# Identity matmuls into an unused bank while TensorE waits, ahead of the expert slots and in the return from them

## What is computed

```
x = x + tanh(g_xattn[0]) * L0_xattn(layernorm(x), ctx, ctx)    # retention, 2 heads
x = x + tanh(g_ffn[0])   * L0_ffn(layernorm(x))                # 8 experts, the best one of each token
x = x + tanh(g_xattn[1]) * L1_xattn(layernorm(x), ctx, ctx)    # 32 heads in 8 groups, causal softmax
x = x + tanh(g_ffn[1])   * L1_ffn(layernorm(x))                # silu(gate) * up, 2 of 4 kept, down
```

## Time and profile before

| | us |
|---|---|
| median of 3 runs | 377.06 (376.61 to 378.37) |
| profiled execution, own time | 379.09 |
| its span, first to last instruction | 377.3 |
| mean granted clock of TensorE | 0.946 of full |
| TensorE busy | 327.8 (87% of the span) |
| VectorE busy | 241.5 (64%) |
| ScalarE busy | 161.4 (43%) |
| GpSimd busy | 102.3 (27%) |

### The profile page before, as it was taken

How to read it: one execution, slowest core, us unless ns; L and a number is a source line. 1 busy time by engine, 2 the same in 40 slices (tenths; PEclk the granted TensorE clock), 3 DMA queues, 4 the chain that set the end, 5 groups by cost and what they waited for, 6 DMA issues and landing times.

```text
span 377.3 us, 4821 instructions
## 1 busy us (share of the span) xinstructions
PE 327.8 (87%) x1526; PEld 208.4 (55%) x1533; DVE 241.5 (64%) x564; ACT 161.4 (43%) x333; POOL 102.3 (27%) x154
## 2 busy tenths in 40 slices
PE   3999785587999727999899999989899999999997
PEld 1485674476888515555544644643534444445885
DVE  4368876683554467889937984992442459778911
ACT  2534361534233312237867665865863233333000
POOL 7203663540000376301441334333450001000000
PEclk9999998578999955999999999999999999999999
DMA  7997000135111126300000000000000000000011
GB/s 247 373 415 202 0 16 2 51 96 174 43 57 56 58 72 232 143 0 7 2 7 0 3 0 9 0 1 9 0 2 1 0 0 2 0 0 0 30 42 42
DMA packets 14025, 22.56 MB, mean 60 GB/s; under 512 B 2049, under 2 KB 11393, under 8 KB 13186
## 3 DMA queue, kind: packets, MB, share of 16 engines
q1 hardware_dynamic: 13234, 20.16, 15.5%
q0 software_dynamic: 768, 2.10, 1.7%
HBM read 15.96 MB, written 6.03 MB: 58 GB/s over the span
## 4 chain that ended last, share of the span: by engine, by line
PE 62%; DVE 19%; ACT 6%; issue 5%; DMA 3%; POOL 3%; SPq 1%; another core or an unknown queue 0%; DVEq 0%; ACTq 0%; POOLq 0%
PE bank L260 46%; DVE mx L1289 6%; PE bank L475 5%; PE bank L443 4%; ACT region L965 3%; PE bank L446 2%; PE bank L276 2%; DVE stats L1035 2%; PE bank L270 2%; ACT s_high L925 1%; POOL rstd L738 1%; DVE x_sb L1075 1%; PE bank L490 1%; DMA x_sb<-in_x_dram 1%; DVE sact L1255 1%
## 5 line engine op out<-in xcount | busy, mean ns | idle before, releaser
L965 ACT ACTIVATE region<-bank,padcol 128x512 f32<-128x512 f32 x96 | 62.4, 695 | 18.1 <-PE bank L260 17.3
L1289 DVE TENSOR_REDUCE mx<-bank 128x2 f32<-128x512 f32 (+1 forms) x96 | 61.3, 684 | 11.2 <-remote 6.3
L260 PE MATMUL bank<-xT,e_gu 128*128 128x512 f32 x128 | 57.6, 594 | 0.5 <-ACT xT L819 0.5
L802 POOL TENSOR_SCALAR_AFFINE_SELECT region<-region 128x1024 f32<-128x1024 f32 x32 | 35.0, 1095 | 81.5 <-ACT region L965 81.4
L260 PE MATMUL bank<-qst,kblk 128*128 128x512 f32 x96 | 46.0, 489 | 0.7 <-DMA qst<-nmT 0.3
L443 PE MATMUL bank<-kblk,qst 128*128 128x512 f32 x96 | 44.5, 482 | 1.6 <-ACT qst L910 0.8
L260 PEld LDWEIGHTS bank<-xT,e_gu 128*128 128x128 f32 x128 | 23.3, 190 | 25.1 <-issue 24.3
L446 PE MATMUL bank<-causb,identb 128*128 128x256 bf16 (+1 forms) x89 | 28.4, 319 | 0.0
L260 PE MATMUL bank<-e_down,region 128*128 128x256 f32 x128 | 27.8, 379 | 0.0
L1075 DVE SCALAR_TENSOR_TENSOR x_sb<-bank,tg,x_sb 128x256 f32<-128x256 f32 x24 | 11.6, 483 | 25.0 <-PE bank L260 24.9
L734 POOL TENSOR_SCALAR veps<-mv 128x1 f32<-128x1 f32 x40 | 10.8, 271 | 61.4 <-DVE mv L1037 59.3
(11 more groups left out here) (177 smaller groups left out, 630.7 us busy)
## 6 DMA issues: line engine op xcount, KB each, us to landing
e_gu<-in_e_gu_dram SPq DMA_DIRECT2D x2, 1408.0 KB, 12.1
x_sorted<-zero SPq DMA_DIRECT2D x1, 1920.0 KB, 9.2
y_sorted<-region SPq DMA_DIRECT2D x15, 128.0 KB, 1.7
x_sb<-in_x_dram SPq DMA_DIRECT2D x4, 256.0 KB, 4.1
ctxT<-in_ctxT_dram SPq DMA_DIRECT2D x2, 512.0 KB, 6.1
e_down<-in_e_down_dram SPq DMA_DIRECT2D x1, 1024.0 KB, 13.9
region<-x_sorted SPq DMA_DIRECT2D x1, 1024.0 KB, 7.5
e_gu<-in_f_gate_dram SPq DMA_DIRECT2D x1, 1024.0 KB, 4.9
```

The lines of the kernel that those rows point to most:

```text
L260: return pe.matmul(dst, lhsT, rhs, start=first, stop=last)
L802: pool.affine_select(out=block, in_=block, compare_op=ALU.is_ge, fill=0.0, base=0, pattern=[[0, 2], [0, PER_GROUP], [1, P]], channel_multi ...
L965: taken(act.activation(dst, src.rearrange("p (h n) -> p h n", n=SEQ - mt * P), ACT.Exp, bias=padcol[:, key:key + 1], scale=float(HD) ** -0 ...
L1289: taken(dve.reduce_max(mx[:, b % 2, nt, quads, q, hg], src, AX), "sa")
```

## The change

A helper `stay_warm` multiplies the identity by the mask, 512 columns, into a bank that no stage uses at that point, so many times; nothing reads the result. It is called in seven places of TensorE's program, with three waits ahead of it. No other engine's program changes.

```diff
+            def stay_warm(bank, n):
+                for _ in range(n):
+                    pe.matmul(banks[bank][:, :], identb[:, :], causb[:, :, :], start=True, stop=True)
...
             pe.wait_ge(sem("routed"), 4)
+            pe.wait_ge(sem("res0_taken"), TILES)
+            stay_warm(7, 7)
             slot_turn(0)
             slot_turn(1)
             pe.wait_ge(sem("gu_split"), 4)
+            stay_warm(7, 4)
             expert = [slot_gate_up(0)]
...
             keys(1, "main")
-            for n in range(QUERIES_AT, QUERIES_AT + 6, 2):
+            pe.wait_ge(sem("sx_taken"), SLOTS)
+            pe.wait_ge(sem("sa_t_taken"), SLOTS)
+            stay_warm(5, 34)
+            for n, gap in ((QUERIES_AT, 2), (QUERIES_AT + 2, 2), (QUERIES_AT + 4, 5)):
                 queries(0, n)
+                stay_warm(5, gap)
             for piece in range(2):
                 stack_piece(0, piece, "main")
+            stay_warm(5, 3)
             for n in range(24):
                 scores(0, n)
```

## The result

The changed kernel took 375.69 us (median of 14, 374.49 to 376.68). The kernel before, run beside it 14 times, took 379.29 us (376.61 to 380.06). The ratio is 0.992 (0.9898 to 0.9942): 3.0 us gained, 2.2 to 3.9 by the interval. Two of the three runs shown ahead of the prediction (376.61, 377.06, 378.37) were among the shortest of this kernel: in all 101 of its timed executions in this study the median was 379.4, and 8 stayed under 377.1.

A forecast was written before the change was run, and what follows sets the result against it. TensorE, 62% of the chain's span, was taken to bound it, at half clock in two places. Terms 1.3 + 3.05 = 4.35 us took the median 377.06 to 372.7, forecast as 373.0; range 371.5 to 375.8.

The forecast's parts named there:

- rival 2: Return: the clock is down again when the queries come, so term 2 is 0; 375.8 us, chance 0.08.
- the sum: Whole kernel: term 1 plus term 2, 1.3 + 3.05 = 4.35, say 4.4 us gained.
- the allowance: From 372.7 to 373.0: a median execution may pay a little less for the clock than the profiled one.
- term 1: Entry of the slot loop: full clock brings the third slot product 1.3 us earlier; bounds 0 and 1.4.
- term 2: Return from the experts: low parts 1.85 us earlier plus 1.2 at the row maxima, 3.05; bounds 1.85 and 3.3.
- The cover of the 34: Return: the 34 matmuls end at 137.4, 0.3 us before the first normalized tile at 137.70.
- the prediction's own signs: Wrong if the 34 end after the first tile; right if no clock under full from 130 to 155.
- Rival 3: Identity products don't hold the clock; the 34 end 5.3 us behind the first tile; 383.4 us, chance 0.06.
- point of decision: TensorE's order before the return's first transpose: it turns slower from 0.24 us per added matmul.
- The price of a matmul: Each added 512-column matmul: 0.23 us at full clock; bounds 0.21 and 0.46.
- the load of slots 2 to 6: Entry: needed by 88.7, there by 88.0, so nothing to pay; cover only 0.7 us.
- just don't bind: Return: the last gathers have landed by 145.2, and residual 6 would want them at 145.6.

The follow-up runs named there:

- return only: Kernel before plus only the return's added matmuls (34, 2, 2, 5, 3), none at the entry; 376.51 us, ratio 0.993.
- block-only kernel: Changed kernel without the 2, 2, 5 and 3 matmuls between the return's steps; the 34 and the entry stay; 376.19 us, ratio 0.991.
- block of 20: Changed kernel with 20 in place of 34 added matmuls in the return; 376.11 us, ratio 0.9926.
- dense tail: Changed kernel with 6 of the 34 matmuls moved ahead of the next batch's keys; 376.06 us, ratio 0.9917; run again 375.55 us, ratio 0.9912.
- block of 58: Changed kernel with 58 in place of 34 added matmuls in the return; 381.4 us, ratio 1.004.
- warm start, first: Changed kernel plus 16 matmuls of zeros by zeros at the start (8 and 2 of 256 columns, 6 of 128); 375.92 us, ratio 0.9905.
- kernel before, again: The kernel before, unedited, run again for the clock of each execution; 379.57 us, ratio 1.0002.

## Why the prediction was wrong in size

The forecast was 373.0 us; 375.69 was measured. It went the way that was forecast and by the mechanism forecast, but the time is 2.7 us off and outside the 371.8 to 374.0 that was given a chance of 0.70. That it lies in the range is luck: the slow end, 375.8, was put there for rival 2, and rival 2 (the clock down when the queries come) did not happen.

**The step that failed** is the last one: "From the median the sum gives 372.7", and then 0.3 more. The median of the three runs, 377.06, is not where this kernel lies: it was 379.0 to 379.6 in every later set, 379.29 beside the changed kernel. Of the 2.7 us, 2.2 come from this base; the sum was 0.75 too large against the medians, and the allowance took 0.3 of that back. The profiled execution's own 379.09, which the text called 2.0 above the median, was an ordinary one; from it the sum had given 374.7. The spread of the three runs was read as a small allowance, when it said that the median could be off by about as much.

**The sum** itself holds in the profile: term 1, 1.3, measured 1.09; term 2, 3.05, measured 3.16. But term 2 agrees in part by luck: the low parts began 1.48 us earlier after the keys, not 1.85, the first row maximum 1.62 and not 1.9, and from there to the negation 1.54 were gained, not 1.2. On the runs the sum is 3.0 to 3.6 us, not 4.35. Two things that the profiles show can make it smaller. The entry's fall isn't in every execution (return only, 5.58 without its matmuls). And the fall near the block can be longer: 75.35 in place of 73.8 for the block-only kernel, whose program is the changed kernel's up to the end of the block. How often each comes was not counted, so that they account for the difference is not shown.

**The cover of the 34** was wrong, and by two of the prediction's own signs it was wrong here: the clock was under full between 130 and 155, and the 34 ended after the first tile, by 0.95 us. "No row shows the clock falling while TensorE works without a gap" was no protection: the earlier trace rows had a mean of 0.59 in a microsecond in which TensorE was busy throughout, after a gap, and in the return it fell at the loose products ahead of the block. Little of the 0.95 reached the end, since the low parts waited only 0.37 us: VectorE's residuals 2 and 3 were the cover, as in the prediction. Rival 3 had this place and its point of decision; its price needed the clock to stay down, and it came back while the added matmuls ran in each of the six profiles with a fall.

**The price of a matmul** was taken as 0.23. Measured, 28 took 6.22 us, 0.22 each, and 0.43 at half clock (131 to 133). The Trainium skill, page "TensorE: Matmul & The Clock Gate", section "Back-to-back issue gap", gives 216 ns for the isolated matmul and 131 ns in a sustained stream of pairs. The trace agrees with the first and not with the second, in a stream of just such pairs.

**The loose products.** The same page, section "A second HAM failure mode: psum-queue depth-cycling", says that short idles between groups of matmuls can bring the clock down. The trace agrees as far as it goes: with no idle over 0.32 us among the last down products and the keys, the clock fell at 130.5, and in both profiles with six matmuls put between them it did not.

**What hides the waits** was right: the three added waits cost nothing in the changed kernel (at most 0.17 us of idle lies between the keys and the block), the load of slots 2 to 6 was in time, and behind the gain VectorE was late next. The gathers "just don't bind" in the changed kernel; they did, by 0.44 us, in the block of 20, where the tile was taken at once, and hardly or not at all in the dense tail's two profiles.

## What to carry to other kernels

Cut two profiles at the same events and compare stretches: here 4.25 us of gain were exact in the stretches changed while the medians moved by anything from 2.7 to 3.6. Take the base of a forecast from more than three runs, or from the profiled execution that the sum was read from. Fill a wait of TensorE as far as the work that it waits for, and not further: past a cover of 0.6 us each matmul was paid in full here, and in one kernel whose fill ended 1.91 us early the clock fell. To keep the clock up through the fill, begin it ahead of the last loose products; here that removed the fall, but a gain in time from it is not shown (0.7 us, within the intervals).

## What was not expected of the hardware

The clock fell while TensorE was reported fully busy (block of 58, 128 to 129: busy 1.00, mean clock 0.58; the microsecond before also 1.00). It came back while nothing but the identity by a causal mask ran (changed, 133.9), and at the start, behind nothing but zeros by zeros, four products took 0.61 us (warm start, first) in place of 1.22 (before). And one kernel's executions differ by 3 us or more on one core, roughly with the mean clock: 376.5 us of span at 0.950, 379.2 at 0.937 (kernel before, again), though at 0.941 alone the spans of the kernel before went from 375.7 to 378.8.
